# Two narrow attentions: the two maxima of a slot placed apart, query stores issued by SyncE, a semaphore of its own for the context, and inner steps written out

## What is computed

```python
x = x + tanh(g_xattn[i]) * xattn_i(layernorm(x), ctx, ctx, ...)
x = x + tanh(g_ffn[i])   * ffn_i(layernorm(x), ...)
```

```python
scores = einsum('bhqd,bhkd->bhqk', Q, K) * scale - slopes[h] * (q_pos - k_pos)
scores = where(mask == 0, -inf, scores)
m = max(scores, axis=-1)
e = exp(scores - m)
attn = e / (1.0 + sum(e, axis=-1))
out = einsum('bhqk,bhkd->bhqd', attn, V) @ W_o.T
```

## Time and profile before

| | |
|---|---|
| median of 3 runs | 1514.68 us (1513.16 to 1520.35) |
| the profiled execution, its own time | 1525.43 us |
| its span | 1523.7 us |
| mean granted TensorE clock | 0.913 of full speed |

### The profile page before, as it was taken

One profiled execution on the slowest core, in us unless ns is written; L12 is line 12 of the kernel. 1 busy time (PEld: TensorE's weight loads), 2 busy tenths in 40 slices (PEclk: granted clock), 3 DMA queues, 4 the chain that ended last, 5 costly groups with the idle time before them and its releaser, 6 DMA issues. The chain is left out here.

```text
span 1523.7 us, 33033 instructions
## 1 busy us (share of the span) xinstructions
PE 1329.0 (87%) x11864; PEld 747.8 (49%) x11872; DVE 1000.3 (66%) x3093; ACT 807.3 (53%) x1190; POOL 763.1 (50%) x727
## 2 busy tenths in 40 slices
PE   5999968827999999999845799999899957999994
PEld 4444454713666666666642344344567723444432
DVE  4988844156766676667475577676455776777766
ACT  3777723335655565656421666567443214666664
POOL 4776613522766676667726445352150057665631
PEclk9999988966999999999955799999799976999997
DMA  4566635436324431440036344330220034233200
GB/s 149 195 226 227 235 125 174 122 128 247 130 82 153 153 132 63 152 153 1 2 51 179 93 114 100 101 86 4 57 46 1 1 72 110 55 62 72 55 6 29
DMA packets 93965, 157.80 MB, mean 104 GB/s; under 512 B 18409, under 2 KB 63620, under 8 KB 90223
## 3 DMA queue, kind: packets, MB, share of 16 engines
q1 hardware_dynamic: 76456, 121.47, 26.7%
q10 hardware_dynamic: 12480, 30.29, 5.5%
q0 software_dynamic: 4880, 4.04, 1.3%
HBM read 99.16 MB, written 50.62 MB: 98 GB/s over the span
## 5 line engine op out<-in xcount | busy, mean ns | idle before, releaser
L2105 DVE CUSTOM_DVE_ANT_0 a_junk<-a_psM,a_madd 128x512 bf16<-128x512 f32 x480 | 313.2, 686 | 109.9 <-issue 105.5
L2048 ACT ACTIVATE a_probs<-a_psE 128x1024 f32<-128x1024 f32 x256 | 262.0, 1024 | 124.0 <-PE a_psE L1908 123.0
L2492 DVE TENSOR_REDUCE a_mx<-a_psM 128x1 f32<-128x512 f32 x236 | 148.2, 669 | 124.5 <-PE a_psM L2316 124.5
L2453 ACT ACTIVATE a_probs<-a_psE 128x1024 f32<-128x1024 f32 x128 | 130.9, 1025 | 85.6 <-PE a_psE L2338 82.3
L2286 POOL TENSOR_TENSOR a_half_sum<-a_probs 128x1024 f32<-128x1024 f32 x64 | 150.9, 2358 | 32.7 <-ACT a_probs L2453 32.7
L1920 PE MATMUL a_psO<-a_probs,narrow_values 128*32 128x256 f32 x2048 | 163.9, 394 | 1.8 <-ACT a_probs L2048 1.1
L1874 PE MATMUL a_psM<-narrow_k_op,narrow_q_op 57*64 57x512 bf16 (+1 forms) x960 | 146.5, 405 | 18.2 <-DMA a_cT<-in_ctxT 10.3
L2334 PE MATMUL a_psE<-a_qT,a_kT 64*128 64x256 f32 x1024 | 133.9, 381 | 0.0
L2350 PE MATMUL a_psO<-a_probs,a_values 128*64 128x256 f32 x1024 | 124.6, 385 | 0.8 <-ACT a_o_raw L2437 0.8
L2474 DVE RECIPROCAL a_o_raw<-a_o_raw 128x256 f32<-128x256 f32 x64 | 111.4, 1741 | 11.0 <-ACT a_o_raw L2437 11.0
L1898 PE MATMUL a_psE<-narrow_q_op,narrow_k_op 60*64 60x256 bf16 (+1 forms) x2048 | 109.4, 287 | 6.6 <-DMA narrow_q_op<-a_max_parts 5.8
(11 more groups left out here) (396 smaller groups left out, 2735.7 us busy)
## 6 DMA issues: line engine op xcount, KB each, us to landing
wide_k<-a_k_stage SPq DMA_DIRECT2D x32, 512.0 KB, 2.6
a_k_part<-wide_k SPq DMA_DIRECT2D x64, 256.0 KB, 3.6
wide_v<-a_v_stage SPq DMA_DIRECT2D x24, 512.0 KB, 3.9
a_kT<-wide_k ACTq DMA_DIRECT2D x6, 2048.0 KB
a_values<-wide_v ACTq DMA_DIRECT2D x6, 2048.0 KB
keys<-a_parts SPq DMA_DIRECT2D x96, 64.0 KB
narrow_k_op<-keys SPq DMA_DIRECT2D x30, 192.0 KB
narrow_q_op<-a_queries SPq DMA_DIRECT2D x28, 192.0 KB
```

The source lines that it names most:

```text
L2048: act.activation(probs[:, head:head + 2, k:k + 2, :], psE[es % 2][:], ACT.Exp).then_inc(exped, 1)
L2105: dve.tensor_tensor_reduce(junk[j][:], max_bank(s, j, first), madd[r][:, t, :], 1.0, -3.0e38, ALU.add, ALU.max, mx[r][:, max_place(h, t):m ...
L2453: act.activation(probs[p % 2][:, :, 2 * half:2 * half + 2, :], psE[half][:], ACT.Exp).then_inc(exped, 1)
L2492: dve.tensor_reduce(mx[r][:, at:at + 1], max_bank(2 * p + t, j, first), AX.X, ALU.max).then_inc(max_read, 1)
```

## The change

- In a slot TensorE now does: the maxima of j=1; scores and then masks of j=0; scores and then masks of j=1; the maxima of j=0; weighing. VectorE takes j=1 first. The count `max_read` is waited for in that order.
- The stores of query chunks 1 to 3 are issued by SyncE: chunk 1 ahead of the first `cross_masks`, chunks 2 and 3 in batches 0 and 1 between the two halves of the maxima. GpSimd splits chunk 1 where it did, and chunks 2 and 3 in batches 0 and 1 between `turned_masks` and the second `split_max`.
- The context tile counts on `context_in`, which TensorE waits for in slot 11, and no longer on `loaded`.
- `steps` calls the six inner batches one by one on every engine.
- In the int8 stage the cast of the slopes (9 x 4096) moves from GpSimd to ScalarE, between `rounding(0)` and `rounding(1)`, behind a wait for its loads.

```diff
@@ NarrowConstants
         pool.tensor_tensor(p2, self.posr[:], p1, ALU.subtract).then_inc(cut, 1)
-        pool.tensor_copy(self.slopes_b[:], self.slopes[:]).then_inc(self.slopes_cut, 1)
+
+    def scalar(self, act):
+        act.wait_ge(self.const_in, 32)
+        act.copy(self.slopes_b[:], self.slopes[:]).then_inc(self.slopes_cut, 1)
@@ narrow_attention
-        n_loads = n_keys + 2 + 1
-        n_first = 2 * N_COPIES + 1
+        n_loads = n_keys + 2
+        n_first = 2 * N_COPIES
...
-        def steps(eng, step):
+        def steps(step):
             step(0, 0, 0)
             step(1, 1, 0)
-            if eng is nc.tensor:
-                for v in range(2, B):
-                    step(v, v % RING, v // RING, inner=True)
-            else:
-                with eng.Fori(0, (B - 2) // RING) as i:
-                    for k in range(RING):
-
-                        step(RING * i + 2 + k, (2 + k) % RING, i + (2 + k) // RING, inner=True)
+            for v in range(2, B):
+                step(v, v % RING, v // RING, inner=True)
             step(B, B % RING, 0)
@@ sync
-                    sp.dma_start(cT[u % RING][:], io["ctxT"][:, u * S2:(u + 1) * S2]).then_inc(loaded[u % RING], 16)
+                    sp.dma_start(cT[u % RING][:], io["ctxT"][:, u * S2:(u + 1) * S2]).then_inc(context_in[u % RING], 16)
...
                 load_queries(1)
+                sp.wait_ge(split, 4)
+                store_queries(sp, 1)
                 cross_masks(0)
...
                         cross_masks(v + 1)
+                    if v + 2 < NCHUNK:
+                        sp.wait_ge(split, 4 * (v + 2))
+                        store_queries(sp, v + 2)
                     maxima(v, 1)
@@ gpsimd
-                for n in range(1, NCHUNK):
-                    split_queries(n)
+                split_queries(1)
...
                         turned_masks(v + 1)
+                    if v + 2 < NCHUNK:
+                        split_queries(v + 2)
@@ tensor, maximum
-                        pe.wait_ge(max_read, v * HEADS * QT + QT * (s - back) + j + 1)
-                    elif s == 1 and j == 0:
+                        pe.wait_ge(max_read, v * HEADS * QT + QT * (s - back) + 2 - j)
+                    elif s == 1 and j == 1:
@@ tensor, step
+                        if take_max:
+                            maximum(v, r, s, 1, not inner and v == 0)
                         if take_exp:
                             if es == 0:
                                 pe.wait_ge(crossed[at], 32 * (w // RING + 1))
-                            score(w, at, es, first)
-                            mask(at, es)
+                            score_waits(w, es, first)
+                            score_half(at, es, 0)
+                            mask_half(at, es, 0)
+                            score_half(at, es, 1)
+                            mask_half(at, es, 1).then_inc(scored, 1)
                         if take_max:
-                            for j in range(2):
-                                maximum(v, r, s, j, not inner and v == 0)
+                            maximum(v, r, s, 0, not inner and v == 0)
...
                                 pe.wait_ge(max_negated, 2 * v + 1)
+                                pe.wait_ge(context_in[r], 16 * (turn + 1))
@@ scalar
-                for n in range(1, NCHUNK):
-                    act.wait_ge(split, 4 * n)
-                    store_queries(act, n)
@@ vector, maximum
-                    for j in range(2):
+                    for j in (1, 0):
                         h = s // 2 * 2 + j
-                        dve.wait_ge(max_scored, v * HEADS * QT + QT * s + j + 1)
+                        dve.wait_ge(max_scored, v * HEADS * QT + QT * s + 2 - j)
@@ layer1_int8, scalar
                 rounding(0)
+                ahead.scalar(act)
                 rounding(1)
```

34 lines of the change are left out of this document (17 added, 17 removed).

## The result

The changed kernel takes 1470.69 us (median, 1466.63 to 1472.73) beside 1517.51 us for the kernel before on the same chip (1513.16 to 1520.81). The ratio is 0.969, 95% interval 0.9653 to 0.9727, so 41 to 53 us less.

What follows compares the result with a forecast made beforehand. TensorE and VectorE taking turns were held to bound the kernel, 1.58 us a slot against 1.35 of work. Terms summing to -43.7 us took the profiled 1525.4 to about 1481.7, hence median 1471; low 1452, high 1492.

Steps and rivals of the forecast that it cites:

- Slots, -34.7: Attention slots of layers two and three: maxima apart in the slot bring it to 1.35 us, net -34.7 us.
- Rival (c): VectorE stays the partner that ends last and the slot remains 1.58 us: 1496 us, chance 0.12.
- Tail, +3.3: Last 13 slots of a stage, without maxima: j=1 scores load behind the j=0 mask, net +3.3 us.
- Rival (d): Row groups issued in halves do not overlap, so the slot takes 1.97 us: 1580 us, chance 0.03.
- Loop, -6.9: Inner steps written out: VectorE's stand at the end of a loop pass goes in both layers, net -6.9 us.
- Rival (e): Straight code stalls as the loop did, once a batch on either engine: +32 us, 1503 us, chance 0.05.
- Start of layer two, -14.4: Query stores off ScalarE: layer two's first score starts at 837 instead of 851.39, -14.4 us.
- Start of layer three, -8.0: Query stores off ScalarE: layer three's first maxima land at 1263.3 instead of 1271.28, -8.0 us.
- Late maxima, +19.4: Maxima of batch halves land late behind moved stores and key loads, in both layers: +19.4 us, between 4 and 42.
- Rival (b): Maxima land late in every half, 1 us beyond the forecast at 28 halves: +20 us, 1491 us, chance 0.20.
- Context semaphore, 0: First maxima wait about 1.3 us less, but GpSimd's masks set the end there: 0 us, bounds 0 and -2.6.
- cast, -2.4: Int8 stage: with the slopes cast on ScalarE, four VectorE quantising steps return to 1.11 us, -2.4 us.

Runs made afterwards that it cites:

- early start: Changed kernel with context tile moved, stores in halves behind the masks, and batch 1's masks and context loaded behind layer two's first maxima: ratio 0.9653.

## Why the prediction was right, point by point

The forecast was 1471 and the median 1471. The mechanism was right, but that the number meets so closely is luck twice. Of seven terms three were off by 3.6 to 4.6 us with signs that largely cancel, and two had their size from other pieces or places than I named. And the forecast took 43.7 off a median of 1514.7, where the measurement took 46.8 off one of 1517.5.

- **What bounds the kernel.** Right. The exchange between TensorE and VectorE was the limit, and the new order alone ends it (25 us with nothing else changed). The 3.1 us a batch that I read off the row of waits were 2.7 by the spacing of the slots.
- **Slots, -34.7, were -39.2.** The coupling that I added (0.62 us a batch) can't be read apart in the traces; with it I had 2.48 gained per batch, and 2.69 came. The rest is the count: what I left out is that the first three slots that score the last batch still have maxima in them, and gain 0.9 us in each stage. Rival (c), a slot that stays at 1.58, did not occur; the margin of 0.02 held. What I said the profile would show, few weight loads waiting for VectorE, did not come: 11 with 4.0 us, at slots that are at their floor.
- **Tail, +3.3, was -0.3.** The failing step is "written as two halves, j=1 scores are loaded behind the j=0 mask". The row groups do not wait for one another in program order. The tail of the changed kernel still has all eight scores together and weighing 0.57 behind them, against 0.56 in the earlier trace rows, and its shortest slots take 1.14 where I had told to look for 1.3. The slots of both tails cost 0.3 in all, not 4.3; the wait for maxima in layer three's tail, of which I had 1 absorbed, shrank by 0.6:

```profile
1039.32 0.42 PE L1903 MATMUL a_psE<-narrow_q_op,narrow_k_op 60*64 60x256 bf16 x8
1039.89 0.42 PE L1924 MATMUL a_psO<-a_probs,narrow_values 128*32 128x256 f32 x4
```

  I had the evidence in the earlier trace rows and used it only for half of what it shows: it says that the groups pass one another, so also that halves and wholes are the same. Rival (d), that the halves would not overlap at all, is out.
- **Loop, -6.9, was -6.8**, in both stages as sized, and it is VectorE's alone. Rival (e) is out: no batch of written-out code stands.
- **Start of layer two, -14.4, was -9.8.** The term mis-sized is "six stores (3 to 5 us by the rows' 0.45 to 0.85 each)"; they took 7.49, two of them 2.69 and 1.96. Behind them the maxima took 5.9 from SyncE's first issue to the last landing, and I had assumed 3.1. Stores moved behind the maxima gave 2.7 of the 4.6 back. What is left fits traffic: from SyncE's first issue to the last landing the maxima took 6.7 there with four of batch 1's loads ahead of them, and 5.9 with its keys and queries alone (early start).
- **Start of layer three, -8.0, was -7.8.** The size is right, the pieces are not, and that is luck. GpSimd was done with its masks at 1226.98, 1.8 us sooner than I had worked out (counted from layer two's last score), and the maxima landed 3.0 after the end of their issue, not 1.05:

```profile
1228.74 2.16 SPq L1665 DMA_DIRECT2D narrow_q_op<-a_max_parts  x3
```

- **Late maxima, +19.4, were +19.5, but in other places.** Batch 0's 6.5 were 2.1, batch 1's 3.8 were 3.1, the later second halves' 5.0 were 1.2, layer two's first halves' 4.7 were 11.6 (3.1 of it half-clock slots), layer three's 1.0 were 2.0. (These add up to 20.0; 0.5 of it I can't set apart from waits that stood before.) My price for keys that are still being moved was too low by more than half, and my price for stores ahead of later halves was too high (10.3 against 5.2). That the sum met is luck of the signs. Rival (b), every half late, is half true: every first half of layer two is, most second halves are not.
- **Context semaphore, 0,** and **cast, -2.4 (was -2.5)**: right, the first confirmed with the part undone. For the cast the expected picture was wrong in one thing: one slow quantising group remains, beside GpSimd's position steps and ScalarE's cast.

The errors were -4.5 (slots), -3.6 (tail) and +4.6 (start of layer two), together -3.5; the rest is small. That is the 47.1 against 43.7.

## What to carry to other kernels

Removing a wait shortens the time between producer and consumer elsewhere, so the room of every transfer in that stretch has to be worked out again: here 39 us gained shrank the room of the first halves' maxima from 7.0 to 6.4 us and brought the big loads closer ahead of them, and the late landings, with those that the moved stores add, cost 19.5 back. Small transfers that an engine waits for were delayed here by the bytes still under way, on both queues; moving one tile of 256 KB from ahead of them to behind them was worth some 10 us by the middles of the intervals, and splitting bulk stores another few, while putting off everything at once only moved the pile to the next small transfer (10.7 us in one slot). Measure the spacing of the slots rather than the sum of waits: the row of waits stayed at 4 us while a batch got 2.7 us shorter.

## What the runs showed of the hardware

- Matmuls of one row group can start ahead of matmuls of the other that precede them in the program: two orders of twelve matmuls gave the same starts within 0.01 us, and two masks of one group started 0.10 us ahead of two scores of the other that stand before them.
- VectorE stands 3.05 to 3.31 us in layer two and 2.3 to 2.6 in layer three (five traces each) at a loop's jump back over three batches of code; written out, the same code has no stand. What it does in that time no record shows.
- A maximum's DMA of 2 KB takes 1.05 us from the end of its issue to the landing in a free stretch; with some 1.5 MB of keys, positions, queries and context issued 3 to 11 us earlier the last piece lands up to 4.4 us after the end of the issue, on either queue.
- A wait of TensorE is followed by some 4.5 us at a granted clock of 0.62 in one place (861.3, after 1.81 us idle) and by full clock (1.00) in another (846.9, after 1.69 us idle). Why one wait costs the clock and the other doesn't stays open.
- Four of VectorE's quantising steps take 3.3 to 3.9 us instead of 1.11 beside GpSimd's position steps (8 x 512, 0.6 to 1.2 us each) or its cast of the slopes. A ScalarE cast of 3.60 us ran beside them too in two traces, and they were no slower than beside GpSimd alone (3.89 and 3.31 against 3.33 and 3.86), but no run had ScalarE's cast without GpSimd's steps.
